# The attention stage of a convolution, attention and feed-forward block: query blocks of 256, maxima of four heads at a time, one bank for sums and weighted values

## The reference, cut to what matters

```python
q = (x @ Wq.T).reshape(b, n, H, HD).transpose(0, 2, 1, 3)
k = (x @ Wk.T).reshape(b, n, H, HD).transpose(0, 2, 1, 3)
v = (x @ Wv.T).reshape(b, n, H, HD).transpose(0, 2, 1, 3)
scores = jnp.einsum('bhqd,bhkd->bhqk', q, k) * SCALE
probs = jax.nn.softmax(scores, axis=-1)
out = jnp.einsum('bhqk,bhkd->bhqd', probs, v)
out = out.transpose(0, 2, 1, 3).reshape(b, n, c)
return out @ Wo.T + bo
```

## Time and profile before

| what | us |
|---|---|
| median of 3 runs | 3147.1 (3146.31 to 3152.84) |
| profiled execution | 3145.05 |
| its span, first to last instruction | 3143.1 |
| first and last score matmul of the attention | 510.4 and 2300.4 |
| the 192 units of the attention | 1791 |
| busy, whole span: TensorE, GpSimd, VectorE, ScalarE | 2819.9, 1849.4, 1900.0, 1548.7 |

### The profile page before, as it was taken

How to read it: one execution, slowest core, us unless ns; L and a number is a source line. 1 busy time by engine, 2 the same in 40 slices (tenths; PEclk the granted TensorE clock), 3 DMA queues, 4 the chain that set the end, 5 groups by cost and what they waited for, 6 DMA issues and landing times. The chain is left out here.

```text
span 3143.1 us, 52348 instructions
## 1 busy us (share of the span) xinstructions
PE 2819.9 (90%) x16784; PEld 1103.9 (35%) x16784; DVE 1900.0 (60%) x2871; ACT 1548.7 (49%) x2582; POOL 1849.4 (59%) x1407
## 2 busy tenths in 40 slices
PE   4988568999899899898998998999849999999999
PEld 3545231333233333332332332332114444444444
DVE  6766248777677677677677678776634333333332
ACT  3322023556556556556556556555634444444433
POOL 2323114899899899899899899999950111110110
PEclk8989776999999999999999999999989999999999
DMA  3333230021111211211211211112020011010110
GB/s 143 105 119 105 93 103 18 21 55 28 65 52 28 70 47 28 74 43 28 79 38 43 67 36 47 48 28 68 1 101 21 21 41 40 20 40 26 34 40 20
DMA packets 68754, 163.87 MB, mean 52 GB/s; under 512 B 13585, under 2 KB 17614, under 8 KB 67470
## 3 DMA queue, kind: packets, MB, share of 16 engines
q1 hardware_dynamic: 68494, 160.67, 16.0%
HBM read 59.20 MB, written 37.75 MB: 31 GB/s over the span
## 5 line engine op out<-in xcount | busy, mean ns | idle before, releaser
L1090 DVE TENSOR_REDUCE b_mxp<-b_mx 128x1 f32<-128x512 f32 x1536 | 1013.4, 684 | 445.7 <-PE b_mx L925 435.2
L1288 ACT ACTIVATE b_ex<-b_st 128x512 f32<-128x512 f32 x1536 | 828.1, 594 | 551.3 <-PE b_st L912 546.8
L1445 POOL TENSOR_TENSOR b_pair<-b_ex 128x512 f32<-128x512 f32 x768 | 987.0, 1296 | 144.1 <-ACT b_ex L1288 134.8
L925 PE MATMUL b_mx<-b_kst,b_qst 96*128 96x512 f16 x1536 | 561.8, 395 | 89.6 <-DVE b_mxp L1090 73.0
L1449 POOL TENSOR_TENSOR b_pair<-b_pair 128x512 f32<-128x512 f32 x368 | 491.5, 1336 | 28.9
L912 PE MATMUL b_st<-b_qst,b_kst 97*128 97x512 f16 x1536 | 473.5, 387 | 35.1 <-issue 17.7
L1665 DVE TENSOR_TENSOR c_gs<-c_g,c_gs 128x512 f16<-128x512 f32 x192 | 132.8, 692 | 481.9 <-ACT c_gs L1738 481.8
L1586 PE MATMUL c_hid<-c_z,c_wi 128*128 128x512 f16 x1728 | 405.6, 380 | 10.8 <-DVE c_z L1658 10.8
L946 PE MATMUL b_pv<-b_ex,b_v 128*32 128x512 f32 x3072 | 413.4, 611 | 1.0 <-ACT b_ex L1288 1.0
L1601 PE MATMUL c_acc<-c_gs,c_wo 128*128 128x512 f16 x1728 | 404.0, 379 | 0.1
L925 PEld LDWEIGHTS b_mx<-b_kst,b_qst 96*128 96x128 f16 x1536 | 130.0, 97 | 682.4 <-DVE b_mxp L1090 570.5
(11 more groups left out here) (159 smaller groups left out, 2897.1 us busy)
## 6 DMA issues: line engine op xcount, KB each, us to landing
a_x<-in_x SPq DMA_DIRECT2D x8, 1536.0 KB, 6.5
a_ob<-a_x SPq DMA_DIRECT2D x8, 1536.0 KB, 7.1
after_conv<-a_ob SPq DMA_DIRECT2D x24, 512.0 KB, 2.6
b_xl<-after_conv SPq DMA_DIRECT2D x8, 1536.0 KB, 6.4
b_qst<-b_staged0q SPq DMA_DIRECT2D x192, 64.0 KB, 2.0
b_kst<-b_staged0k SPq DMA_DIRECT2D x192, 64.0 KB, 2.0
b_v<-b_vstaged SPq DMA_DIRECT2D x24, 512.0 KB, 3.0
b_xr<-after_conv SPq DMA_DIRECT2D x8, 1536.0 KB, 6.6
```

Source lines behind the costliest of these rows:

```text
L925: nc.tensor.matmul(mx[item % 2][:, :], qst[g][0:MAXROW, h, t * P:(t + 1) * P], kst[g][0:MAXROW, h, half * BANK:(half + 1) * BANK], start=T ...
L1090: nc.vector.reduce_max(mxp[h % 2][:, t, half:half + 1], mx[item % 2][:, :], AX_X).then_inc(mx_taken, 1)
L1288: nc.scalar.activation(ex[u % 2 * HG + s][:, e * BANK:(e + 1) * BANK], st[(SCORES * u + n) % NST][:, :], ACT.Exp, scale=SCALE).then_inc(ex ...
L1445: nc.gpsimd.tensor_tensor(both[:, :], e[:, 0:BANK], e[:, BANK:NPIX], ALU.add).then_inc(pair_ready, 1)
```

## The change

A unit becomes one group of four heads, 256 queries and four key tiles. Two units make a block x (12 blocks in an image), so the count of units stays 24. In detail:

- **Maxima.** A wave is four matmuls, one for each head, of 32 rows (the high halves alone), 512 keys and 128 queries. They lie in four row groups of TensorE and write four banks, which are now one tile `mx`. VectorE reduces all four banks with one instruction (`take_wave`). A unit has two waves, one at the end of each half (e = 0 and 1). Four waves serve a block, and they run six waves ahead (AHEAD), so that the last wave of block x stands at the end of unit 2x - 2 and its reduction at the start of unit 2x - 1.
- **Shift rows.** VectorE reduces, transposes and negates the block's 2 x 4 x 128 maxima (`top`, `top_turned`, `shift`); TensorE's transpose and ScalarE's `row` go. SyncE's `load_rows` waits for them in unit 2x - 1 and issues 16 DMAs for block x, each of one or three rows of 32 numbers (64 bytes). Unit 2x begins with scores that wait for all 16.
- **Scores.** A fill of a bank is two matmuls of 256 columns instead of one of 512; there are two banks `st` instead of three.
- **Weighing and sums.** The bank `pv` holds the weighted values of 256 queries and their sums beside one another. GpSimd's second addition goes; the matmuls with ones come in every unit, in two parts. `weigh` runs one or two halves behind the scores, at the end of each half. ScalarE's move, VectorE's inversion and product and the split of the result come once in two units instead of once in four, with half as many columns except for the move.
- **Layer norm.** The reciprocal of the standard deviation is done on transposed numbers, in three steps instead of four quarters.
- **Prologue.** The 64 items of the first maxima shrink to six waves; block 0's `load_rows` stands ahead of the third `stack`.

The core of the diff:

```diff
+    IU = 24
+    BLOCKS = IU // 2
+    QUERIES = NPIX // 4
+    WAVES = 2 * IU
+    AHEAD = 6
+    NST = 2
+    ROWS = 16 * 4 * (P // ROW)
...
-            def load_row(turn, g, h):
-                sp.wait_ge(row_ready, turn + 1)
-                sp.dma_start(qst[g][MAXROW:MAXROW + 1, h, :], mr[h % 2][:, :]).then_inc(row_loaded[h], 16)
+            def load_rows(b, x):
+                sp.wait_ge(turned, TURN * (BLOCKS * b + x + 1))
+                g, q0 = x // 4, x % 4 * QUERIES
+                for a in range(P // ROW):
+                    for w in range(2):
+                        for h0, h1, at in ((0, HG - 1, HG - 1), (HG - 1, HG, 0)):
+                            q = q0 + w * P + a * ROW
+                            sp.dma_start(qst[g][at * HEAD:at * HEAD + 1, h0:h1, q:q + ROW],
+                                         shift[a * ROW + w * HG + h0:a * ROW + w * HG + h1, :]
+                                         ).then_inc(row_loaded[x % 2], 16)
...
+            def unit(b, u, qkv=True):
+                if u == 2 and not in_prologue(b):
                     stack(b, 2)
+                if u % 2 and has_wave(b, 2 * u - 1):
+                    load_rows(*((b, (u + 1) // 2) if u < IU - 1 else (b + 1, 0)))
                 if u == 12 and qkv:
                     stack(b + 1, 0)
                 if u == 18 and qkv:
...
+            def scores(b, u, e, s):
+                x, kh = u // 2, u % 2
+                g, q0 = x // 4, x % 4 * QUERIES
+                n = HG * e + s
+                depth = P if s == HG - 1 else 3 * HEAD + 1
+                if kh == 0 and n == 0:
+                    pe.wait_ge(row_loaded[x % 2], ROWS * (BLOCKS // 2 * b + x // 2 + 1))
+                wait(pe, exp_ready, FILLS * (IU * b + u) + n + 1 - NST)
+                for j in range(2):
+                    kt = 4 * kh + 2 * e + j
+                    last = nc.tensor.matmul(st[n % NST][:, j * QUERIES:(j + 1) * QUERIES],
...
+            def wave(b, h):
+                number = WAVES * b + h + AHEAD
+                x, w = (h + AHEAD) // 4, (h + AHEAD) % 4
...
+                wait(pe, mx_taken, number)
+                for s in range(HG):
+                    rows = slice(s * HEAD, (s + 1) * HEAD)
+                    last = nc.tensor.matmul(mx[:, s, :], qst[g][rows, s, q0 + t * P:q0 + (t + 1) * P],
+                                            kst[g][rows, s, half * BANK:(half + 1) * BANK],
+                                            start=True, stop=True, tile_position=(s * HEAD, 0))
+                last.then_inc(mx_ready, 1)
...
+                for e in range(2):
+                    scores(b, u, e, 0)
...
+                    scores(b, u, e, 1)
...
+                        scores(b, u, e, 2)
...
+                    scores(b, u, e, 3)
+                    if lagging(b, u, 2 - e):
+                        weigh(*before(b, u, 2 - e), 1 - e)
+                    if has_wave(b, 2 * u + e):
+                        wave(b, 2 * u + e)
...
+            def take_wave(b, h):
+                number = WAVES * b + h + AHEAD
+                x, w = (h + AHEAD) // 4, (h + AHEAD) % 4
+                dve.wait_ge(mx_ready, number + 1)
+                nc.vector.reduce_max(mxp[x % 2][:, w // 2, :, w % 2], mx[:, :, :], AX_X
                                      ).then_inc(mx_taken, 1)
...
-                    if u % 2 and maxima:
-                        pool.wait_ge(pair_ready, STEPS * unit_no + s + 1)
-                        nc.gpsimd.tensor_tensor(both[:, :], both[:, :], pair[s][:, :], ALU.add
-                                                ).then_inc(pair_added, 1)
```

More of the change, by code:

```diff
@@ L717, in schedule @@
             for u in range(FIRST, IU):
-                unit(last, u, norm=False, qkv=False, maxima=u < IU - UNITS)
+                unit(last, u, norm=False, qkv=False)
             epilogue(last)
@@ L724, in bank_of, with has_wave, before, lagging @@
         def bank_of(m, i):
[L726 to L737, removed]
+            return pv if in_prologue(m) and i % 2 else pj
+        def has_wave(b, h):
+            return not (isinstance(b, int) and b == n_images - 1 and h + AHEAD >= WAVES)
+        def before(b, u, lag):
+            return (b, u - lag) if u >= lag else (b - 1, IU + u - lag)
+        def lagging(b, u, lag):
+            return not (isinstance(b, int) and b == 0 and u < lag)
         @block.sync
@@ L754, in stack @@
                     wait_both(sp, (lo_staged, 12 * m + 4 * g + 4), (v_staged, 6 * m + 2 * g + 2))
[L756 to L759, removed]
+                wait(sp, pv_ready, 2 * (IU * (m - 1) + IU // GROUPS * (g + 1)))
+                for h in range(HG):
+                    low, high = [r for r in range(4) if r != h and r != (0 if h == HG - 1 else HG - 1)]
+                    for dst, part, parts in ((qst, 0, (0, 1, 0)), (kst, 1, (0, 0, 1))):
+                        for r, s in zip((h, low, high), parts):
                             sp.dma_start(dst[g][r * HEAD:(r + 1) * HEAD, h, :],
@@ L782, in prologue @@
                 load_x(1)
+                sp.wait_ge(rows_set, 4 * GROUPS)
+                load_rows(0, 0)
                 stack(0, 2)
[L784 to L793, removed]
+            def unit(b, u, qkv=True):
+                if u == 2 and not in_prologue(b):
                     stack(b, 2)
+                if u % 2 and has_wave(b, 2 * u - 1):
+                    load_rows(*((b, (u + 1) // 2) if u < IU - 1 else (b + 1, 0)))
                 if u == 12 and qkv:
@@ L827, in _ @@
             for u in range(FIRST, IU):
-                unit(last, u, qkv=False, maxima=u < IU - UNITS)
+                unit(last, u, qkv=False)
             epilogue(last)
@@ L871, in project_part @@
                 if kind < 2:
[L872 removed]
+                    for n in range(9 * piece // pieces, 9 * (piece + 1) // pieces):
                         (a, b), k = PARTS[n // KC], n % KC
@@ L899, in out_project @@
                                             start=n == 0, stop=n == 8)
[L900 to L927, removed]
@@ L933, in weigh @@
             def weigh(b, u, e):
-                g, w = u // UNITS, u % UNITS
+                x, kh = u // 2, u % 2
                 unit_no = IU * b + u
[L937 to L950, removed]
@@ L966, in sum_up @@
+                last.then_inc(pv_ready, 1)
+                pe.wait_ge(pair_ready, HG * (unit_no + 1))
+                for s in range(HG):
+                    last = nc.tensor.matmul(pv[s * HEAD:(s + 1) * HEAD, QUERIES:BANK], ones[:, :],
+                                            pair[u % 2][s][:, e * QUERIES:(e + 1) * QUERIES],
+                                            start=False, stop=kh == 1 and e == 1,
+                                            tile_position=(0, s * HEAD))
                 last.then_inc(sum_ready, 1)
@@ L984, in prologue @@
                 for h in range(HALVES):
                     mean(1, h)
-                pe.wait_ge(row_of_ones, 3)
-            def unit(b, u, out_proj=True, norm=True, qkv=True, maxima=True, load=False):
-                g, w = u // UNITS, u % UNITS
-                group = GROUPS * b + g + 1
-                image = b + 1 if g == GROUPS - 1 else b
-                lag = (b, u - 1) if u else (b - 1, IU - 1)
-                lagging = not (isinstance(b, int) and b == 0 and u == 0)
+                wait(pe, *free[id(pv)])
@@ new lines, in unit @@
+            def unit(b, u, out_proj=True, norm=True, qkv=True, load=False):
+                def beside(n):
+                    if n == 5 and u >= FIRST and qkv:
+                        stage_low(b + 1, u - FIRST)
+                    if u % 2 and n >= 5 and lagging(b, u, 3):
+                        invert_sum(b, (u - 3) // 2, n - 5)
+                    if u % 2 == 0 and n == 1 and lagging(b, u, 4):
+                        attended(b, (u - 4) // 2)
+                    if load and u >= IU - 2 and n == 7:
+                        for k in range(KC):
+                            centre(b + 2, u - IU + 2, k)
@@ L1422, in prologue, with unit @@
+                    nc.gpsimd.memset(kst[g][0:1, HG - 1, :], 1.0).then_inc(rows_set, 1)
+                    pool.wait_ge(rows_set, 4 * g + 4)
                 for h in range(HALVES):
                     fold_x(1, h)
-            def unit(b, u, out_proj=True, norm=True, maxima=True, load=False, **_flags):
-                unit_no = IU * b + u
-                started = not (isinstance(b, int) and b == 0 and u < 4)
-                for s in range(STEPS):
+            def unit(b, u, out_proj=True, norm=True, qkv=True, load=False):
+                if norm and u in (0, 1):
+                    fold_squares(b + 1, u)
+                for s in range(HG):
```

476 lines of the change are left out of this document (218 added, 258 removed).

## The result

The changed kernel takes 3753.45 us (median of 4, 3745.24 to 3763.35) against 3149.97 (3146.31 to 3153.38). The ratio is 1.192, with a 95% interval of 1.188 to 1.195. The forecast was 3840 us in a range of 3570 to 4080. The profiled execution is the slowest of the four (3763.35 us); its span is 3761.4 us.

A forecast was written before the change was run, and what follows sets the result against it. The prediction took TensorE and GpSimd as nearly full before, and SyncE's row issues as the new wait: 96 blocks of 25.6 us plus 54 make 2512 against 1791 (+721), prologue -27, so 3840 us, range 3570 to 4080.

The forecast's parts named there:

- The mechanism: Each block's 16 row-load issues on SyncE outlast the one unit TensorE has meanwhile; TensorE stands about 6.6 us a block.
- The chain: From a block's last wave to the next block's first scores: reduction, small operations, 16 issues and landing, together 14.5 us.
- TensorE's unit: Scores, maxima waves, weighing and sums, projections sum to 7.5 us; two gaps from two score banks make it 7.9.
- The clock: Half clock for 7.5 us after each block's idle stretch; first unit 11.1 us, block 25.6 instead of 22.4.
- the third rival: Chain as worked out but the clock stays high, 22.4 us a block, 3610 us in all; chance 0.17.
- The additions for each image: Beside the blocks: late rows behind `stack`, the square root's table loads and loop turns, 54 us over the stage.
- The total: Stage 2512 us against 1791, +721; prologue -27; whole kernel 3840 us; chance of the forecast itself 0.56.
- the prologue: Before the image loop: it loses its 64 maxima, so block 0's rows are in place earlier, -27 us.
- The first rival: The row loads are hidden behind TensorE's unit and the kernel is faster, 2975 us; chance 0.07.

The follow-up runs named there:

- rows_32: The changed kernel with 32 DMAs for a block instead of 16, one head each, same bytes: 4747.65 us, 1.508 of the kernel before.
- rows_8: The changed kernel with 8 DMAs for a block instead of 16, each four strided rows of one head, same bytes: 3149.12 us, 1.000 of the kernel before.
- lead_ten: The changed kernel with waves ten ahead instead of six and two shift buffers, 16 DMAs issued a block earlier: 3055.70 us, 0.970 of the kernel before.
- warm_wait: The changed kernel with 24 matmuls, result overwritten, ahead of each wait for the shift rows: 3697.29 us, 1.175 of the kernel before.
- lead_ten_rows_8: The changed kernel with waves ten ahead, two shift buffers and 8 DMAs for a block: 3003.91 us, 0.953 of the kernel before.

## Why the prediction was right, point by point

- **The mechanism** was right, and rows_32, rows_8 and lead_ten confirm it from three sides: more issues, fewer issues, the same issues earlier. 95 waits of 6.85 us on average were measured, some 95 of 6 to 7 were forecast. In the list of waits it is the fourth and not, as forecast, the largest; it is TensorE's largest. About half of the 95 lie between 6 and 7 us; seven of 0.8 and 21 of 8 to 11 happen to average to it.
- **The chain** was forecast at 14.5 us from the end of a block's last wave and came out at 14.5: reduction 2.28 forecast and 2.29 measured, small operations 0.55 and 0.56 without gaps, issues and landing 11.3 and 11.4. The last agreement is of two small misses: the pitch was 0.64 instead of 0.66, and from the start of the last issue (1246.55) to the scores 1.7 us passed, where 1.4 and TensorE's 0.1 were forecast.
- **TensorE's unit** was forecast at 7.9 us and measured at 7.8, a wave at 0.3 and measured at 0.33. The drain on a change of tiling mode that the Trainium skill names (TensorEngine Tiling (Array Packing), Key Properties) is within these numbers: a wave's 0.33 us is 0.11 more than one matmul of 512 columns takes, and the trace shows no idle time around it.
- **The clock** was mis-sized. The mechanism holds (1.6 us a block, warm_wait; with the added matmuls a plain block takes 22.3 us, and the third rival had 22.4), but half clock ended 3.8 us after work began again and not 7.6 to 8.3, as in the earlier trace rows. The first unit takes 9.4 us, not 11.1, the block 23.9 and not 25.6: some 160 us less over 96 blocks.
- **The additions for each image** were too small: 54 us over the stage were forecast. The scores run from 478.4 to 2919.4, 2441 us, and 96 blocks of 23.9 are 2294, so about 147 were lost beside the plain blocks. A part of it is in the row above: a `stack` adds 3.3 us to a block. The sum had 1 us, because it thought TensorE's first unit to be 11.1 us long. In the turn from 1066.73 to 1377.14 twelve blocks take 23.6 us more than twelve plain ones: 10.7 in the three blocks with a `stack` and nearly all of the rest in five other blocks around the layer norm and the loop's turn. What each of those waits for wasn't taken apart.
- **The total** is nearer than its parts, and that is luck: some 160 us too much for the blocks and 93 too little for the additions leave 71 in the stage. It grew by 652 us (forecast 721), and the prologue shrank by 33 (forecast 27). The first score matmul runs at 478.4, against 511.3 in the earlier trace rows; the 510.4 of the table ahead is its weight load:

```profile
L899 PE MATMUL b_st<-b_qst,b_kst x3072: 270/273/421, 478.4 to 2919.4; 97*128 97x256 f16 x192
```

- **The first rival** was priced at 2975 us. lead_ten_rows_8, in which the rows are out of the way, takes 3004. The unit is as priced; its stage takes 1670 us (489.5 to 2159.7) where the rival had 1650, as units with layer norm and the loop's turn are somewhat longer than the 206 us an image allowed, and its prologue gives 21 us and not 27.
- **A sum of the third rival** is off: a `stack` late by 4.2 us three times, 3 us for the square root in each of seven images and 12 for the turns are 121, not 131, so its price was 3600 us. The range doesn't depend on it.

## What to carry to other kernels

Count the DMAs of a step, not their bytes: in these runs each copy within the core's memory costs its issuing queue about 0.55 to 0.7 us, and when the last of them gates the next step, that sum stands in the chain. Put it against the time between the last input and the first use before a row is cut into pieces, and give it one more stage of lead if it doesn't fit; here that one block of lead decided between 19% slower and 3% faster. Read waits block by block before you compare them with a forecast: in rows_8 the average wait lay where it was expected, and most single waits did not. A good change can hide behind a bad wait: the row groups (195 us) and GpSimd's relief (73 us) showed their worth only when the queue was out of the way.

## What the runs showed that I had not expected

The length of an issue does not follow the number of its pieces. SyncE's issues by line in rows_8 (four rows, 64 bytes each), in rows_32 (one row) and in the changed kernel (three rows and one row in turn), as shortest, median, longest ns:

```profile
L758 SPq DMA_DIRECT2D b_qst<-b_shift x768: 492/492/742, 462.6 to 2289.9; - x192
```

```profile
L759 SPq DMA_DIRECT2D b_qst<-b_shift x3072: 497/589/1977, 462.0 to 3882.8; - x192
```

```profile
L759 SPq DMA_DIRECT2D b_qst<-b_shift x1536: 509/675/1105, 462.1 to 2903.7; - x192
```

Four strided rows are issued in 492 ns. One row takes 589 in rows_32, behind another one-row issue, but about 510 to 520 in the changed kernel, where the issues of three rows between take 675 to 686; the 675 of the last line is theirs. So rows_8 gained by fewer issues and by shorter ones. What sets the length is open.

The other thing is how long half clock stays after a stop. It ended 3.8 us after work began again in the plain blocks and about 8 in the earlier trace rows, after shorter idle stretches. It is not that a stop which returns each 24 us is followed by a shorter one: in the same run the block of 1144.92 had half clock from 1139.4 to 1153.1, 8.2 us beyond the start of work, and the block of 1275.46 to 1279.4, 3.9 us, although its wait was the longer of the two (9.85 against 8.27 us).

```profile
1139.40:1153.10 13.70, 6.66 (x41) 2.54 (x42) 2.57 (x5) 4.12 (x7) 0.32 (x1) 0.50 0.01 0
```

What decides it is open. Three stretches of one kernel were too few to price it.
